# Routed tiles of an MoE layer: four strips and a 32x32 block transpose on VectorE in place of a TensorE transpose and a ScalarE copy

## What is computed

```
logits = flat @ router_w.T
topk_p, topk_i = top_k(softmax(logits), 2);  topk_w = topk_p / sum(topk_p)
out = sum over e of (square(relu(flat @ w_fc[e].T)) @ w_proj[e].T) * combine[:, e]
out = out + square(relu(flat @ shared_fc.T)) @ shared_proj.T
x = layernorm(x + out)
```

## Time and profile before

| what | us |
|---|---|
| median of three timed runs | 492.7 |
| span of the profiled execution | 498.7 |
| first load of a routed tile issued on SP | 327.1 |
| first and last `up` on PE | 332.5, 466.3 |
| last scatter issued on POOL | 471.2 |
| PE busy in the span | 453.9 (91%) |
| DVE, ACT, POOL busy in the span | 356.7, 354.5, 315.1 |

### The profile page before, as it was taken

The page is one execution under the profiler, slowest core; times in us unless marked ns, Lnnn a source line. Parts: engine busy times, 40 slices in busy tenths (PEclk is TensorE's granted clock), DMA queues, the critical chain, the costliest instruction groups (busy, mean ns, idle before and its releaser), DMA issues.

```text
span 498.7 us, 7644 instructions
## 1 busy us (share of the span) xinstructions
PE 453.9 (91%) x2184; PEld 293.6 (59%) x2184; DVE 356.7 (72%) x873; ACT 354.5 (71%) x557; POOL 315.1 (63%) x285
## 2 busy tenths in 40 slices
PE   8997999999999988798898898489999999999983
PEld 5332444444344333455576675389999999899721
DVE  5898999999999999998688964353333333455246
ACT  3989999999999999815455555327667667566537
POOL 4754789999999999845566666604555455555421
PEclk9998999999999999989799999979999999999997
DMA  8031246654343434001111111131222222222095
GB/s 274 8 122 43 86 146 213 216 196 151 130 153 131 151 133 148 3 1 33 39 45 43 45 43 47 46 94 51 72 65 81 71 60 58 60 57 67 11 324 182
DMA packets 41193, 48.56 MB, mean 97 GB/s; under 512 B 5616, under 2 KB 25266, under 8 KB 41152
## 3 DMA queue, kind: packets, MB, share of 16 engines
q1 hardware_dynamic: 35792, 39.07, 23.8%
q0 software_dynamic: 5216, 8.70, 5.6%
q10 hardware_dynamic: 144, 0.31, 0.2%
HBM read 19.17 MB, written 29.11 MB: 97 GB/s over the span
## 4 chain that ended last, share of the span: by engine, by line
PE 40%; POOL 22%; DVE 16%; issue 8%; ACT 7%; DMA 2%; another core or an unknown queue 2%; DVEq 0%; POOLq 0%; SPq 0%; ACTq 0%
POOL memory_feat L495 17%; PE routed_ph L1500 13%; PE routed_po L1513 12%; PE dispatch_sph L998 4%; PE dispatch_spo L1008 3%; POOL memory_feat L503 2%; DVE memory_prod L769 2%; DVE memory_y_raw L778 2%; POOL memory_prod L518 2%; PE memory_nsum L620 1%; ACT finish_xo L1714 1%; PE routed_px L1488 1%; PE dispatch_plr L969 1%; DVE memory_feat L769 1%
## 5 line engine op out<-in xcount | busy, mean ns | idle before, releaser
L495 POOL TENSOR_TENSOR memory_feat<-memory_feat,memory_p_tok 128x1024 f32<-128x1024 f32 x64 | 125.9, 2063 | 17.1 <-ACT memory_feat L390 14.2
L620 PE MATMUL memory_nsum<-memory_feat,tri 128*128 128x512 f32 x256 | 118.1, 604 | 6.3 <-ACT memory_last_rows L403 2.4
L1476 POOL DMA_INDIRECT pick_scratch<-routed_ob,routed_xg x71 | 71.6, 1008 | 75.1 <-DVE routed_ob L1597 56.7
L1192 POOL DMA_INDIRECT table_scratch<-dispatch_xrow,dispatch_slot x64 | 61.9, 967 | 40.9 <-PE dispatch_sph L998 18.9
L620 PEld LDWEIGHTS memory_nsum<-memory_feat,tri 128*128 128x128 f32 x256 | 47.8, 192 | 65.1 <-issue 56.2
L1546 ACT ACTIVATE routed_rel<-routed_ph 128x512 f32<-128x512 f32 x71 | 42.3, 597 | 47.7 <-PE routed_ph L1500 46.7
L1513 PE MATMUL routed_po<-routed_w2c,routed_hid 128*128 128x128 f32 x568 | 71.3, 276 | 1.2 <-DVE routed_ob L1597 0.7
L1500 PE MATMUL routed_ph<-routed_xs,routed_w1c 128*128 128x256 f32 (+1 forms) x368 | 71.1, 337 | 1.2 <-DVE routed_w2c L1583 0.9
L1597 DVE TENSOR_SCALAR routed_ob<-routed_po,routed_xg 128x128 f32<-128x128 f32 x71 | 22.6, 347 | 69.2 <-issue 49.6
L769 DVE TENSOR_TENSOR memory_prod<-memory_nsum,memory_query 128x1024 f32<-128x1024 f32 x58 | 68.8, 1216 | 1.9 <-PE memory_nsum L620 1.8
L1513 PEld LDWEIGHTS routed_po<-routed_w2c,routed_hid 128*128 128x128 f32 x568 | 67.0, 192 | 1.9 <-issue 1.1
(11 more groups left out here) (192 smaller groups left out, 694.6 us busy)
## 6 DMA issues: line engine op xcount, KB each, us to landing
table_scratch<-memory_blank SPq DMA_DIRECT2D x68, 260.0 KB, 2.6
finish_pick<-pick_scratch SPq DMA_DIRECT2D x16, 256.0 KB, 6.0
routed_xg<-table_scratch SPq DMA_DIRECT2D x25, 130.0 KB
w<-w_up SPq DMA_DIRECT2D x9, 256.0 KB, 2.7
w<-w_down SPq DMA_DIRECT2D x9, 256.0 KB, 3.1
x_tok<-x SPq DMA_DIRECT2D x4, 512.0 KB, 3.7
out<-finish_xo SPq DMA_DIRECT2D x7, 256.0 KB, 2.3
routed_xg<-table_scratch SPq DMA_DIRECT2D x21, 65.0 KB
```

The costliest lines, as they stand in the source:

```text
L495: nc.gpsimd.tensor_tensor(v, v, pv, ALU.mult).then_inc(wfeat_done, 1)
L620: last = nc.tensor.matmul(nsum[:, o:o + 512], tri[:], feat[:, i % U, h, q * 512:(q + 1) * 512], start=True, stop=True)
L1192: nc.gpsimd.indirect_dma_start(out=table, in_=xrow[:, r, n, :], in_offset=None, out_offset=bass.IndirectOffsetOnAxis(ap=slot[:, r, n:n + 1 ...
L1476: nc.gpsimd.indirect_dma_start(out=pick_dram, in_=ob[:, u, h, :], in_offset=None, out_offset=bass.IndirectOffsetOnAxis(ap=xg[:, t % XU, h, ...
```

## The change

The load of a tile becomes five DMAs. Four bring strips of 32 channels: strip j goes to partitions 32j to 32j + 31 of `xb`, in blocks of 32 rows, so that each 32 x 32 block stands at the place where its transpose belongs. A piece of a strip is 32 floats, 128 bytes, of one row. The fifth brings the two last columns of the rows to `mark`, in pieces of 8 bytes, and counts on a semaphore of its own, `marked`. DVE's block transpose, new function `turn`, turns each 32 x 32 block of `xb` in one instruction per tile, from SBUF to `xs` in SBUF. `turn` and its PSUM bank leave PE, `keep_x` leaves ACT, and the wait before `shared(6)` goes. On DVE `turn(t+2)` stands between `weights(t+3)` and `ob(t)`; it waits for the four strips of tile t + 2 and for `up(t)`.

```
     HALVES = ROWS // P
     U = 4
     XU = 8
+    SQ = 32
+    STRIPS = D // SQ
     with ExitStack() as c:
         def sb(name, shape, dt=F32):
             return c.enter_context(nc.sbuf_tensor("routed_" + name, shape, dt))
...
         def sem(name):
             return outer.enter_context(nc.semaphore("routed_" + name))
 
-        xg = sb("xg", [P, XU, HALVES, RW])
+        xb = sb("xb", [P, XU, ROWS])
+        mark = sb("mark", [P, XU, HALVES, RW - D])
         xs = sb("xs", [P, 2, ROWS])
         w1c = sb("w1c", [P, U, FF])
         w2c = sb("w2c", [P, U, FC, D])
...
         ph = [ps(f"ph{i}", [P, FC * ROWS]) for i in range(2)]
         ps("unused", [P, FC * P])
         po = ps("po", [P, FC * P])
-        px = ps("px", [P, FC * P])
         loaded = [sem(f"loaded{u}") for u in range(XU)]
+        marked = [sem(f"marked{u}") for u in range(XU)]
         scattered = [sem(f"scattered{u}") for u in range(U)]
         turned = sem("turned")
-        x_kept = sem("x_kept")
         w_ready = sem("w_ready")
         up_done = sem("up_done")
         rel_done = sem("rel_done")
...
                 if not early(t, XU):
                     sp.wait_ge(scattered[u], passes(t - XU))
                 n = height(t)
-                sp.dma_start(xg[:, t % XU, 0:n], table[bass.ds(first, n * P), :].rearrange("(h p) c -> p h c", p=P)
-                             ).then_inc(loaded[t % XU], 16)
+                rows = table[bass.ds(first, n * P), :]
+                for j in range(STRIPS):
+                    sp.dma_start(xb[j * SQ:(j + 1) * SQ, t % XU, 0:n * P].rearrange("a (i b) -> a i b", b=SQ),
+                                 rows[:, j * SQ:(j + 1) * SQ].rearrange("(i a) b -> a i b", a=SQ)).then_inc(loaded[t % XU], 16)
+                sp.dma_start(mark[:, t % XU, 0:n], rows[:, D:].rearrange("(h p) c -> p h c", p=P)).then_inc(marked[t % XU], 16)
             tiles(lambda: None, load)
 
         def gpsimd(pool):
...
                 for h in range(height(t)):
                     nc.gpsimd.indirect_dma_start(
                         out=pick_dram, in_=ob[:, u, h, :], in_offset=None,
-                        out_offset=bass.IndirectOffsetOnAxis(ap=xg[:, t % XU, h, D:D + 1].bitcast(U32), axis=0),
+                        out_offset=bass.IndirectOffsetOnAxis(ap=mark[:, t % XU, h, 0:1].bitcast(U32), axis=0),
                         bounds_check=2 * NTOK - 1, oob_is_err=False).then_inc(scattered[u], 16)
             tiles(lambda: None, body)
 
         def tensor(pe):
-            def turn(t, u):
-                pe.wait_ge(loaded[t % XU], 16 * (t // XU) + 16)
-                if not early(t, 1):
-                    pe.wait_ge(x_kept, t)
-                for h in range(height(t)):
-                    last = nc.tensor.transpose(px[:, h * P:(h + 1) * P], xg[:, t % XU, h, 0:D], ident[:])
-                last.then_inc(turned, 1)
-
             def up(t, u):
                 s = u % 2
-                pe.wait_ge(x_kept, t + 1)
+                pe.wait_ge(turned, t + 1)
                 pe.wait_ge(w_ready, t + 1)
                 n = height(t) * P
                 per = FC // height(t)
...
                 last.then_inc(down_done, 1)
 
             def front():
-                turn(0, 0)
-                turn(1, 1)
                 up(0, 0)
 
             def body(t, u):
                 if not beyond(t, 1):
                     up(t + 1, (u + 1) % U)
-                if not beyond(t, 2):
-                    turn(t + 2, (u + 2) % U)
                 down(t, u)
             tiles(front, body)
 
         def scalar(act):
-            def keep_x(t, u):
-                act.wait_ge(turned, t + 1)
-                if not early(t, 2):
-                    act.wait_ge(up_done, parts(t - 1))
-                n = height(t) * P
-                nc.scalar.copy(xs[:, u % 2, 0:n], px[:, 0:n]).then_inc(x_kept, 1)
-
             def rectified(t, u):
                 s = u % 2
                 for n in range(parts(t), parts(t + 1)):
...
                     nc.scalar.activation(hid[:, s, o:o + FC * P], rel[:, n % 2, :], ACT.Square).then_inc(hid_done, 1)
 
             def front():
-                keep_x(0, 0)
-                keep_x(1, 1)
                 rectified(0, 0)
                 squared(0, 0)
 
             def body(t, u):
                 if not beyond(t, 1):
                     rectified(t + 1, (u + 1) % U)
-                if not beyond(t, 2):
-                    keep_x(t + 2, (u + 2) % U)
                 if not beyond(t, 1):
                     squared(t + 1, (u + 1) % U)
             tiles(front, body)
...
                 nc.vector.tensor_copy(w2c[:, u], w2[:, bass.ds(e, 1)].rearrange("p o c d -> p (o c) d")
                                       ).then_inc(w_ready, 1)
 
+            def turn(t):
+                dve.wait_ge(loaded[t % XU], 16 * STRIPS * (t // XU + 1))
+                if not early(t, 2):
+                    dve.wait_ge(up_done, parts(t - 1))
+                n = height(t) * P
+                nc.vector.transpose(xs[:, t % 2, 0:n], xb[:, t % XU, 0:n]).then_inc(turned, 1)
+
             def front():
                 for t in range(3):
                     weights(t, t)
+                    if t < 2:
+                        turn(t)
 
             def body(t, u):
                 if not beyond(t, 3):
                     weights(t + 3, (u + 3) % U)
+                if not beyond(t, 2):
+                    turn(t + 2)
                 dve.wait_ge(down_done, t + 1)
+                dve.wait_ge(marked[t % XU], 16 * (t // XU + 1))
                 if not early(t, U):
                     dve.wait_ge(scattered[u], passes(t - U))
                 for h in range(height(t)):
-                    last = nc.vector.tensor_scalar(ob[:, u, h, :], po[:, h * D:(h + 1) * D], xg[:, t % XU, h, D + 1:D + 2],
+                    last = nc.vector.tensor_scalar(ob[:, u, h, :], po[:, h * D:(h + 1) * D], mark[:, t % XU, h, 1:2],
                                                    None, ALU.mult)
                 last.then_inc(kept, 1)
             tiles(front, body)
 
         return RoutedStage(sync=sync, scalar=scalar, gpsimd=gpsimd, tensor=tensor, vector=vector,
                            scattered=[(scattered[t % U], passes(t)) for t in range(TILES - U, TILES)],
-                           x_kept=x_kept, rel_done=rel_done, banks=parts(TILES), kept=kept)
+                           rel_done=rel_done, banks=parts(TILES), kept=kept)
 
 
 def finish(nc, outer, rou, ident, y_all, eps, warm, pick_dram, out):
...
 
             shared(4)
             shared(7)
-            pe.wait_ge(rou.x_kept, TILES)
             shared(6)
             pe.wait_ge(rou.rel_done, rou.banks)
             for g in range(4):
```

More of the change, by code:

```diff
@@ L1531, in scalar @@
         def scalar(act):
[L1532 to L1537, removed]
             def rectified(t, u):
```

16 lines of the change are left out of this document (5 added, 11 removed).

## The result

The changed kernel takes 506.58 us (median of 4 runs, 506.08 to 507.47), the kernel before 492.72 beside it (491.91 to 492.95): 13.9 us more, a ratio of 1.030 [1.028, 1.032]. The forecast was 512.2 in a range of 494 to 520.

A forecast was written before the change was run, and what follows sets the result against it. `routed` looked bound by PE; after the change SP's issue queue would set the pace, moving the last `up` from 466.29 to 485.76. That +19.5 us on 492.7 gave 512.2 us, range 494 to 520.

The forecast's parts named there:

- The mechanism: SP's queue in `routed`: five issues make a load 3.43 us (3.39 in half tiles), so PE waits for strips; chance 0.55.
- the listed signs: In `routed`: 230 issues about 0.57 apart, hardly a scatter wait, 1.4 us waits per half tile, last `up` near 486, PE under 60%.
- The price of an issue: On SP's queue: each added issue costs 0.57 us, counting DMA, two register instructions and gaps; 46 x 4 come to 105 us.
- the bounds: For the 0.57 per issue on SP: 0.47 from back to back issues with fixed addresses, 0.61 from the load of x.
- the second rival: SP's issues cost 0.47 to 0.53, as with fixed addresses, if register work is shared; 493.9 to 504.9 us; chance 0.13.
- Landing: After the last tile's fourth strip is issued on SP, its data lands 2.53 us later, at 485.31.
- At the start: First `up` in `routed` needs four more issues and `turn(0)` follows `weights(0)`: about 0.4 us, hidden if SP sets the end.
- The first, hidden issues: SP's waits and eight buffers of lead hide the issues, full tiles take 3.52; 5.1 us faster, 487.6 us; chance 0.10.
- The third rival, the clock: PE, busy 53% in half tiles, drops to clock 0.50, a half tile needs 3.58; up to 517.6 us; chance 0.18.
- The fourth, the pieces: Small pieces bound the DMA engines in full tiles, 4.6 us per tile, 1.2 over SP's 3.43; 542 us; chance 0.04.

The follow-up runs named there:

- the 100-byte run: Changed kernel with one DMA in place of the four strips, moving pieces of 100 bytes (1280 in a full tile); 484.79 us, 0.9885 of before.

## Why the prediction was right, and where its sum was off

**The mechanism** was the forecast's: SP's issue queue sets the pace in the half tiles. 230 issues, no scatter waits, DVE and PE waiting 1.2 to 1.3 us in a half tile (1.4 forecast): these are in the profile as the prediction listed them, and the runs with two, six and five issues on two queues show it. Besides the distance of the issues, two of the listed signs missed. The last `up` was to come near 486, 158.6 us after the first load; it came 154.1 after it. And PE is busy 66% in the half tiles where I had said under 60%. That the load is 3.11 and not 3.39 is not enough for this: with the prediction's 1.79 of PE's work it would still be 58%. In the half tile shown PE counts as busy from 439.33 to 441.38, 2.05 us, and the lower clock near 455 adds to the share: outside those 4 us it is 19.94 of 32, 62%.

**The sum** gave +19.5 us; the trace has +15.0, the runs +13.9. Three terms were off, in both directions:
- *The price of an issue*: 0.57 forecast, 0.50 measured. I took the DMA instruction's 377 ns from the line that was changed; a strip's takes 317. 183 issues x 0.07 = 12.8 us too much. The price lay inside the bounds (0.47 to 0.61), in the span of the second rival, at whose 0.50 the sum is 512.2 - 12.8 = 499.4. That rival's reason, shared register work, is not what happened: each of the 184 strips has its register operation and its move in the rows above.
- *Long issues*, which the sum didn't have. Clean, 25 x 3.16 + 20 x 3.11 = 141.2 us from the first load's first issue to the last load's; measured, 468.36 - 317.92 = 150.44. So 9.2 us came from issues that took longer than their form and from shorter stalls in the queue (below). This took most of the first error back. That the total lies as near the forecast as it does is in part luck: the sum had no such term.
- *Landing*: 2.53 forecast from the second load; for the last tile 471.70 - (468.36 + 2.02) = 1.32, 1.2 less. The rows, the end of the stage in the changed kernel:

```profile
468.36 2.02 SPq L1472 DMA_DIRECT2D routed_xb<-table_scratch  x4
...
471.70 0.31 DVE L1573 STREAM_TRANSPOSE routed_xs<-routed_xb 128x128 f32<-128x128 f32 x1 [2.58 <-DMA routed_xb<-table_scratch]
...
472.06 1.16 PE L1497 MATMUL routed_ph<-routed_xs,routed_w1c 128*128 128x128 f32 x8 [1.34 <-DVE routed_xs L1573]
```

With the measured terms 19.5 - 12.8 + 9.2 - 1.2 = 14.7.

**The parts.** PE's full tile is 3.51 (3.52 forecast). The block transpose took 0.44 us for 256 columns and 0.31 for 128, where 0.46 and 0.35 were taken; DVE had room, and no waiter but the late strips showed. At the start I had taken 0.4 us more; the first `up` came 322.35 - 317.92 = 4.4 us after the first load, where before it was 332.5 - 327.1 = 5.4. Nothing of that reaches the end, as SP sets it. PE waits for strips from the sixth half tile on and not from about the third: after the full tiles SP's lead was about 6.2 - 1.2 = 5 us, where I had summed 3 at most.

**The rivals.** The first, hidden issues at 487.6, is near what the runs with one issue for the four strips took, 485.98 and 484.79: had the issues been hidden, the change would have gained about 1%. The rule of the Trainium skill behind it, that the time to initiate a DMA "is usually small relative to the DMA itself" ("DMA: Bandwidth & Descriptors", "Issuing engines are not separate DMA queues"), is not what decides here: what one issue takes, 0.50 us, is smaller than the landing (1.32 above), but five of them in one queue are more than a half tile. The same section says that issuing from several engines saves only that time; here that time was the bound, and moving one strip to ScalarE gave 12.7 us. The third rival, the clock, showed in 3.4 us at 0.50 and is no cause: the late half tiles at clock 1.00 have the same period. The fourth, the pieces, fell with the 100-byte run.

## What to carry to other kernels

An engine that shows no busy time can be the next bound: before splitting a transfer, price the issue by the distance between issues in the queue's own timeline, multiply, and compare with the tile's period stage by stage, since the same five issues were hidden under a tile of 3.5 us and not under one of 2.0. A new layout by strips pays where its issues fit, so it can be used in the tall tiles alone (485.64 against 491 and 507), and part of the issues can go to another engine's queue. Merging issues helps only as far as the merged form is itself cheaper: time it first.

## What the hardware showed that was not expected

**The price of an issue goes by its form.** DMA instructions with an address from a register took 0.32 us for 32 partitions, whether in 4 or 8 pieces of 128 bytes per partition or in 1 or 2 of 520; 0.60 to 0.61 for 64 partitions in pieces of 256 bytes, the same in full and half tiles. One over all 128 partitions took 0.34 with one row per partition (half tiles of the kernel before and of the run with one issue for four), 0.38 with two rows that lie 128 rows apart (full tiles of before), 0.55 with two neighbouring rows (full tiles of one issue for four), and 0.55 with 5 or 10 pieces of 100 bytes. The runs with one issue for four, pieces of 512 bytes first, shortest/median/longest ns:

```profile
L1471 SPq DMA_DIRECT2D routed_xb<-table_scratch x46: 337/548/598, 319.1 to 444.0; - x46
```

```profile
L1473 SPq DMA_DIRECT2D routed_xb<-table_scratch x46: 548/554/1242, 318.3 to 447.6; - x46
```

So two of 64 partitions hold the queue longer than one of 128. Why, no run here tells. The mark's DMA, the same each time, also goes by what stands ahead of it in the queue: in full tiles 0.39 after a strip, 0.46 after 64 partitions, 0.62 after the pieces of 100 bytes.

**Long issues.** Seven issues of the changed kernel took 0.76 to 1.56 us. One, the last strip of this load on SP's queue:

```profile
330.90 2.70 SPq L1472 DMA_DIRECT2D routed_xb<-table_scratch  x4
333.78 0.39 SPq L1474 DMA_DIRECT2D routed_mark<-table_scratch  x1
```

Four strips took 2.70 instead of 1.82. The DMA queues in the stretch 332 to 333.7 hold one transfer of the kind "instruction":

```profile
q1 hardware_dynamic: 745, 0.09, 38.6%
q0 software_dynamic: 30, 0.06, 9.9%
q8 instruction: 1, 0.02, 3.5%
```

In the 1.8 us after it there is none, and each of the other six long issues stands beside such a packet in the same way. That SP stood still until its next instructions were there is a guess from this; it was not tested, as no run varied the code alone. The kernel before has eight such packets between its first load and its last, and no issue over 0.43; as SP mostly waits there, that doesn't decide it. It matters only where the queue has no slack: the seven were 6.1 us over their form, and together with shorter stalls they were the 9.2 us above, a term that a price per issue does not contain.
